# Two attention layers on 32 images: second layer normalised before its product, with a new order of work

## The reference

```
# layer 0, for each image
h    = group_norm(x, 32 groups) * gn_w + gn_b
q,k,v = split(qkv_w @ h + qkv_b)            # 128 x 1024 each
attn = softmax(q.T @ k * C**-0.5)           # 1024 x 1024
x1   = x + proj_w @ (v @ attn.T) + proj_b
# layer 1
q = Wq @ x1 + bq ; k = Wk @ x1 + bk         # 16 x 1024 each
v = Wv @ x1 + bv                            # 128 x 1024
y = gamma * (v @ softmax(q.T @ k).T) + x1
```

## Time and profile before

| | |
|---|---|
| median of three runs | 1635.73 us (1635.26 to 1635.94) |
| profiled execution, own time | 1633.07 us |
| its span, first to last instruction | 1630.8 us |
| granted TensorE clock, mean | 0.988 |
| busy share PE / DVE / ACT / POOL | 93% / 79% / 74% / 76% |
| DMA moved | 305 MB, 187 GB/s over the span |

### The profile page before, as it was taken

How to read it: one execution, slowest core, us unless ns; L and a number is a source line. 1 busy time by engine, 2 the same in 40 slices (tenths; PEclk the granted TensorE clock), 3 DMA queues, 4 the chain that set the end, 5 groups by cost and what they waited for, 6 DMA issues and landing times.

```text
span 1630.8 us, 43555 instructions
## 1 busy us (share of the span) xinstructions
PE 1519.8 (93%) x16777; PEld 1102.4 (68%) x16777; DVE 1289.7 (79%) x2499; ACT 1209.0 (74%) x1697; POOL 1247.4 (76%) x1036
## 2 busy tenths in 40 slices
PE   3789999999999999999999999999999999999975
PEld 1557777767777677776767777677677777767754
DVE  2478888888888888888888888888888888887854
ACT  1467887777777777777777777877777877777753
POOL 3998888887888887787888788788878888877600
PEclk9999999999999999999999999999999999999987
DMA  1689999999999999999999999999999999999974
GB/s 47 117 143 200 196 198 201 209 192 201 195 201 204 198 196 196 197 198 192 203 203 204 203 190 204 198 198 205 190 203 194 195 205 197 203 189 186 195 137 97
DMA packets 1081437, 305.19 MB, mean 187 GB/s; under 512 B 1068273, under 2 KB 1068945, under 8 KB 1081233
## 3 DMA queue, kind: packets, MB, share of 16 engines
q1 hardware_dynamic: 1080080, 302.41, 106.1%
q10 hardware_dynamic: 1152, 0.00, 0.0%
HBM read 17.13 MB, written 16.78 MB: 21 GB/s over the span
## 4 chain that ended last, share of the span: by engine, by line
PE 48%; ACT 22%; DVE 16%; issue 10%; POOL 2%; DMA 1%; SPq 1%; ACTq 0%; POOLq 0%; DVEq 0%
DVE nmax L498 10%; ACT scores L402 9%; ACT prob L397 8%; PE mixed L710 7%; PE mixed L712 7%; PE mixed L711 7%; PE scores L671 6%; PE bank_w L778 4%; PE scores L673 4%; PE scores L672 4%; PE scores L696 3%; PE bank_t L731 2%; ACT v_head L452 2%; PE bank_w L768 2%; DVE qk L563 1%
## 5 line engine op out<-in xcount | busy, mean ns | idle before, releaser
L710 PE MATMUL mixed<-v_head,pt 128*128 128x129 f16 x4096 | 722.6, 223 | 4.5 <-DMA pt<-rows 4.3
L712 PE MATMUL mixed<-v_head,pt 128*128 128x129 f16 x4096 | 722.5, 220 | 0.0
L711 PE MATMUL mixed<-v_tail,pt 128*128 128x128 f16 x4096 | 722.2, 219 | 0.0
L498 DVE TENSOR_REDUCE nmax<-scores 128x1 f32<-128x1024 f32 x512 | 602.4, 1216 | 52.6 <-PE scores L696 32.3
L305 POOL TENSOR_TENSOR rows<-prob,rows 128x1024 f16<-128x1024 f32 x256 | 545.5, 2131 | 21.3
L402 ACT ACTIVATE scores<-scores,nmax 128x1024 f32<-128x1024 f32 x256 | 278.6, 1088 | 279.4 <-DVE nmax L498 279.4
L300 POOL TENSOR_SCALAR rows<-prob 128x1024 f16<-128x1024 f32 x256 | 267.9, 1046 | 227.3 <-ACT prob L397 210.8
L512 DVE SCALAR_TENSOR_TENSOR rows<-scores,rows 128x1024 f16<-128x1024 f32 x256 | 313.6, 1225 | 153.3 <-ACT rows L409 153.2
L711 PEld LDWEIGHTS mixed<-v_tail,pt 128*128 128x128 f16 x4096 | 407.0, 99 | 2.7
L710 PEld LDWEIGHTS mixed<-v_head,pt 128*128 128x128 f16 x4096 | 400.2, 98 | 7.0 <-DMA pt<-rows 6.6
L712 PEld LDWEIGHTS mixed<-v_head,pt 128*128 128x128 f16 x4096 | 398.1, 97 | 0.0
(11 more groups left out here) (90 smaller groups left out, 1847.0 us busy)
## 6 DMA issues: line engine op xcount, KB each, us to landing
x_raw<-in_x_dram SPq DMA_DIRECT2D x32, 512.0 KB, 4.8
out_dram<-y SPq DMA_DIRECT2D x64, 256.0 KB, 3.0
pt<-rows SPq DMA_TRANSPOSE x512, 4.9
w_qkv<-in_L_conv_qkv_w_dram SPq DMA_DIRECT2D x3, 64.0 KB, 3.8
b_qk<-in_L_conv_bk_dram SPq DMA_DIRECT2D x8, 0.1 KB, 1.9
b_qk<-in_L_conv_bq_dram SPq DMA_DIRECT2D x8, 0.1 KB, 1.6
w_proj<-in_L_conv_proj_w_dram SPq DMA_DIRECT2D x1, 64.0 KB, 3.5
w_v<-in_L_conv_Wv_dram SPq DMA_DIRECT2D x1, 64.0 KB, 3.4
```

What stands on the lines that cost most here:

```text
L498: nc.vector.reduce_max(nmax[layer][:, t:t + 1], scores[layer][:, :], AX.X, negate=True).then_inc(maxed[layer], 1)
L710: mm(mixed[l][:, 0:C + 1], head, vh[:, im.p, m, 0:C + 1], start=(m == 0), stop=False)
L711: mm(mixed[l][:, 0:C], head, vt[:, im.p, m, :], start=False, stop=False)
L712: done = mm(mixed[l][:, 0:C + 1], tail, vh[:, im.p, m, 0:C + 1], start=False, stop=(m == TILES - 1))
```

## The change

- **Layer 1 rows are normalised when they are split.** `exponent1` also writes out the row sum; VectorE scales it down by 4096 and takes the reciprocal (`invert1`, two instructions of one column, behind both row maxima); `head_row1` waits for it and uses it as scale, and `tail_row1` does too. Both are issued in two halves of 512 columns, and each half of `score1` waits for its half of the tail before it.
- **Layer 1's product has channels in partitions.** `attend1` has v1 as the stationary side and the rows as the moving side, so `norm` and `back` fall away for layer 1, with the column of ones, and `y_out` adds `x1b` straight to PSUM.
- **Layer 0** keeps both; its turned tile now lands in a free part of `mixed[0]`, and `attend0` of the next tile waits for `x1_done`. `x_bias` and `xb` are gone: `x1_out` adds bias and `x_raw` itself. `x_raw` has five buffers and is loaded earlier.
- **The order** of the list on every engine is new. TensorE: scores 1, scores 0, turn back, attend 1, projections, attend 0, q and k. ScalarE: exponent 1, head 1, the outs of v, qk1 and v1, and only then exponent 0 and norm. VectorE: max 1, max 0, invert 1, exp bias, x1, tail 1, y, the tails, invert 0, group norm. The waits `adds_done` and `evicted_here` on TensorE are gone. In the new list v is in steps 0 and 2, qk1 in 1 and 3, its copies in 3 and 4, v1 in 6 and 7, q and k in 2, 4, 5 and 0, statistics in 4 and 5, group-norm products in 6 and 7, and `h_head` in 7.

The diff, cut; the waits of `qk_project`, `v_project`, `qk1_project` and `gn_product` were fitted to the new order, and `attend0` is `attend` for layer 0.

```diff
+X_BUFS = 5
...
+TURNED = slice(2 * C, 3 * C)
...
+PIECES = 2
...
-SCORE = (-1, 12)
-EXP = (0, 13)
-SWING = (1, 13)
-ATTEND = (3, 16)
-ADD = (4, 17)
-QK_AT = (-5, -4, -3, 0)
-GN_AT = (-10, -9)
-V_AT = (1, 2)
-QK1_AT = (7, 11)
-V1_AT = (12, 14)
-TURNED = (slice(0, C), slice(C, 2 * C))
-FIRST_IT, LAST_IT = -2, IMAGES + 2
+LOAD_X, STATS, GN_AT, ROOT_AT = -22, (-20, -19), (-18, -17), -12
+H_FULL, H_HEAD, H_TAIL = -9, -9, -7
+QK_AT, QK_SPLIT = (-6, -4, -3, 0), (-5, -3, -2, 2)
+V_AT, QK1_AT, QK1_COPY, V1_AT = (0, 2), (9, 11), (11, 12), (14, 15)
+EXP, SWING, ATTEND, BACK = (0, 13), (1, 13), (3, 16), 4
+X1_BIAS, STORE = 12, (20, 24)
+FIRST_IT, LAST_IT = -3, IMAGES + 2
...
             def load_x(im):
-                if im.at_least(2):
-                    sp.wait_ge(x_biased, im.n - 1)
-                    sp.wait_ge(h32_done, im.n - 1)
-                    sp.wait_ge(h_head_done, im.n - 1)
-                sp.dma_start(x_raw[:, im.p, :], x_img[im.n]).then_inc(x_loaded[im.p], 16)
+                if im.at_least(X_BUFS):
+                    sp.wait_ge(x1_done, (im.n - X_BUFS + 1) * TILES)
+                sp.dma_start(x_raw[:, im.n % X_BUFS, :], x_img[im.n]).then_inc(x_loaded[im.n % X_BUFS], 16)
...
-            def x_bias(im):
-                if isinstance(im.n, int) and im.n == 0:
-                    pool.wait_ge(setup_dve, SETUP_DVE_ALL)
-                if im.at_least(2):
-                    pool.wait_ge(x1_done, im.n * TILES - TILES)
-                    stand_apart()
-                nc.gpsimd.tensor_scalar(xb[:, im.p, :], x_raw[:, im.p, :], bias0[:, 0:1], 1.0, ALU.add,
-                                        ALU.mult).then_inc(x_biased, 1)
...
             def exponent1(im, t):
                 act.wait_ge(maxed[1], im.n * TILES + t + 1)
                 nc.scalar.activation(scores[1][:, :], scores[1][:, :], ACT.Exp,
-                                     bias=nmax[1][:, t:t + 1], scale=1.0).then_inc(exped[1], 1)
+                                     bias=nmax[1][:, t:t + 1], scale=1.0,
+                                     accum_out=rsum[:, t:t + 1]).then_inc(exped[1], 1)
 
             def head_row1(im, t):
                 if early := two_before(im, t):
                     act.wait_ge(swung[1][early[1] % RING], swings(*early))
-                act.wait_ge(exped[1], im.n * TILES + t + 1)
-                nc.scalar.activation(rows[1][:, t % 2, 0, :], scores[1][:, :], ACT.Copy,
-                                     scale=P_UP).then_inc(row_headed[1], 1)
-
-            def norm(l, im, t):
-                act.wait_ge(inverted[l], im.n * TILES + t + 1)
-                nc.scalar.activation(normal[l][:, :], mixed[l][:, 0:C], ACT.Copy,
-                                     scale=rinv[l][:, t:t + 1]).then_inc(normed[l], 1)
+                act.wait_ge(inverted[1], im.n * TILES + t + 1)
+                for piece in range(PIECES):
+                    cols = slice(piece * N // PIECES, (piece + 1) * N // PIECES)
+                    nc.scalar.activation(rows[1][:, t % 2, 0, cols], scores[1][:, cols], ACT.Copy,
+                                         scale=rinv[1][:, t:t + 1]).then_inc(row_headed[1], 1)
+
+            def norm(im, t):
+                act.wait_ge(inverted[0], im.n * TILES + t + 1)
+                nc.scalar.activation(normal[:, :], mixed[0][:, 0:C], ACT.Copy,
+                                     scale=rinv[0][:, t:t + 1]).then_inc(normed, 1)
...
-                        if im := at(it, k, QK1_AT[h] + 1):
+                        if im := at(it, k, QK1_COPY[h]):
                             qk1_copy(im, h)
                     if tile := tile_at(it, k, EXP[1]):
                         exponent1(*tile)
                         head_row1(*tile)
-                    if tile := tile_at(it, k, EXP[0]):
-                        exponent0(*tile)
...
+                    if tile := tile_at(it, k, EXP[0]):
+                        exponent0(*tile)
+                    if tile := tile_at(it, k, ATTEND[0]):
+                        norm(*tile)
...
-                    if im := at(it, k, -7):
+                    if im := at(it, k, H_HEAD):
                         h_head_out(im)
-                    for l in range(2):
-                        if tile := tile_at(it, k, ATTEND[l]):
-                            norm(l, *tile)
...
 
-            def invert(l, im, t):
-                dve.wait_ge(attended[l], im.n * TILES + t + 1)
-                nc.vector.reciprocal(rinv[l][:, t:t + 1], mixed[l][:, C:C + 1]).then_inc(inverted[l], 1)
+            def invert0(im, t):
+                dve.wait_ge(attended[0], im.n * TILES + t + 1)
+                nc.vector.reciprocal(rinv[0][:, t:t + 1], mixed[0][:, C:C + 1]).then_inc(inverted[0], 1)
+
+            def invert1(im, t):
+                dve.wait_ge(exped[1], im.n * TILES + t + 1)
...
+                                        ALU.mult).then_inc(lowered, 1)
+                dve.wait_ge(lowered, im.n * TILES + t + 1)
+                nc.vector.reciprocal(rinv[1][:, t:t + 1], rsum_down[:, t:t + 1]).then_inc(inverted[1], 1)
 
...
-                dve.wait_ge(row_headed[1], im.n * TILES + t + 1)
-                nc.vector.scalar_tensor_tensor(out=rows[1][:, t % 2, 1, :], in0=scores[1][:, :], scalar=P_UP,
-                                               in1=rows[1][:, t % 2, 0, :], op0=ALU.mult,
-                                               op1=ALU.subtract).then_inc(row_tailed[1], 1)
+                for piece in range(PIECES):
+                    cols = slice(piece * N // PIECES, (piece + 1) * N // PIECES)
+                    dve.wait_ge(row_headed[1], (im.n * TILES + t) * PIECES + piece + 1)
+                    nc.vector.scalar_tensor_tensor(out=rows[1][:, t % 2, 1, cols], in0=scores[1][:, cols],
+                                                   scalar=rinv[1][:, t:t + 1], in1=rows[1][:, t % 2, 0, cols],
+                                                   op0=ALU.mult, op1=ALU.subtract).then_inc(row_tailed[1], 1)
 
             def x1_out(im, t):
                 cols = slice(t * C, (t + 1) * C)
-                if t == 0:
...
-                nc.vector.tensor_tensor(x1[:, im.p, cols], bank_t[:, TURNED[0]], xb[:, im.p, cols],
-                                        ALU.add).then_inc(x1_done, 1)
+                dve.wait_ge(turned, im.n * TILES + t + 1)
+                if t == 0 and im.at_least(2):
+                    dve.wait_ge(x1_biased, im.n - 1)
+                nc.vector.scalar_tensor_tensor(out=x1[:, im.p, cols], in0=mixed[0][:, TURNED], scalar=bias0[:, 0:1],
+                                               in1=x_raw[:, im.n % X_BUFS, cols], op0=ALU.add,
+                                               op1=ALU.add).then_inc(x1_done, 1)
...
                 h, cols = t // PER_HALF, slice(t * C, (t + 1) * C)
+                dve.wait_ge(attended[1], im.n * TILES + t + 1)
...
-                nc.vector.tensor_tensor(y[:, h, (t % PER_HALF) * C:(t % PER_HALF + 1) * C], bank_t[:, TURNED[1]],
-                                        x1b[:, im.p, cols], ALU.add).then_inc(y_done, 1)
+                nc.vector.scalar_tensor_tensor(out=y[:, h, (t % PER_HALF) * C:(t % PER_HALF + 1) * C],
+                                               in0=mixed[1][:, 0:C], scalar=1.0 / P_UP, in1=x1b[:, im.p, cols],
+                                               op0=ALU.mult, op1=ALU.add).then_inc(y_done, 1)
...
                 for k in range(8):
-                    if tile := tile_at(it, k, EXP[1]):
-                        row_max(1, *tile)
+                    here = tile_at(it, k, EXP[1])
+                    if here:
+                        row_max(1, *here)
                     if tile := tile_at(it, k, EXP[0]):
                         row_max(0, *tile)
+                    if here:
+                        invert1(*here)
+                    if tile := tile_at(it, k, EXP[0]):
                         exp_bias(*tile)
-                    for l in range(2):
-                        if tile := tile_at(it, k, ADD[l]):
-                            dve.wait_ge(turned[l], tile[0].n * TILES + tile[1] + 1)
-                    if tile := tile_at(it, k, ADD[0]):
+                    if tile := tile_at(it, k, BACK):
                         x1_out(*tile)
-                    if tile := tile_at(it, k, ADD[1]):
+                    if here:
+                        tail_row1(*here)
+                    if tile := tile_at(it, k, ATTEND[1]):
                         y_out(*tile)
-                    if tile := tile_at(it, k, EXP[1]):
-                        tail_row1(*tile)
-                    for l in range(2):
-                        if tile := tile_at(it, k, ATTEND[l]):
-                            invert(l, *tile)
                     for h in range(2):
                         if im := at(it, k, V_AT[h]):
...
-                        if im := at(it, k, -12 + h):
+                    if tile := tile_at(it, k, ATTEND[0]):
+                        invert0(*tile)
...
```

(51 more changed lines are left out.)

143 lines of the change are left out of this document (66 added, 77 removed).

## The result

The changed kernel takes 1672.6 us (1671.95 to 1673.29, four runs) beside 1635.49 us for the one before: a ratio of 1.0227, with a 95% interval of 1.021 to 1.0245. It is slower by 37.1 us. The forecast was slower, 1654 us, by 18.5; direction and range hold, the size is half of what came.

What follows compares the result with a forecast made beforehand. Light steps were bound by a ring of maxima, exponentials and head, projection steps by TensorE. The new ring adds 0.64 us an image, + 19 over some 30 images, + 1 for the ends: 1654 us, range 1606 to 1678.

Steps and rivals of the forecast that it cites:

- The ring: Chain from maxima through `invert1`, `head_row1` and `exponent0` back: 5.33 us; through layer 1's tail and `exponent1`: 5.43 plus read-out.
- T: The moment at which VectorE starts `invert1`, behind both maxima, 1.13 us after the start of max 0.
- the outs ahead of `exponent0`: ScalarE's copies of v, qk1 and v1: no waiting, but 0.49 us added for v and v1, 0.66 for qk1.
- the three copies of step 2: On ScalarE, `norm`, the copy of q and k and `qk1_copy` delay the next step's `exponent1`; step forecast at 6.11 us.
- the ends: Layer 1 alone at the end: 0.1 to 0.2 us more in each of 16 steps, last tile saves about 1; together + 1.
- The pointer: On ScalarE's head, taking the scale from a column costs up to 0.09 us; 0.08 was taken.
- The read-out a: Writing out the row sum after `exponent1` on ScalarE: estimated 0.16 us, bounds nothing to 0.36.
- a = 0: Rival: reading out the row sum costs nothing; 47.68 us an image, 1629 us; chance 0.13.
- A full instruction (0.36): Rival: reading out the row sum costs a full instruction with its wait; 50.01 us an image, 1699 us; chance 0.06.
- Late turned tiles: Rival: GpSimd's waits for the DMA move to ScalarE's head, 0.70 us an image; 1675 us; chance 0.11.
- TensorE gives back its turns: Rival: TensorE is the bound and 28 us of turns back are won; 1608 us; chance 0.19.
- The limit: With SyncE's queue waiting 22.8 of 800 us and transfers unchanged, time can't fall by more than 2.9%, to 1589.

Runs made afterwards that it cites:

- the short copy: Changed kernel with the first of two copies of layer 1 queries (L422) cut to 64 of 512 columns, save for the first two images: 1662.27 us.
- the half swings: Layer 1's transpose cut to the head rows: in the changed kernel without normalising, 1584.74 us; in the kernel before, 1635.32 us.
- the never normalised kernel: Changed kernel with constant 4096 as scale of head and tail, no wait for `invert1`, which is left out: 1612.96 us.

## Why the direction was right and the size half

**The ring, right.** The structure stood as forecast: `head_row1` waits for `invert1` in all steps, TensorE is busy for 45.99 of 49.09 us (94%, forecast under 95%), steps are 5.87 to 6.37 us. `exponent0` to max 0 was 1.56 and is 1.56; max 0 to T 1.13 and is 1.15. Five of the eight steps agree within 0.07: 7, 0, 4, 5 and 6 with 6.11, 5.91, 5.87, 6.14 and 6.28 against 6.14, 5.87, 5.92, 6.21 and 6.30; step 1 is 0.09 over, 6.08 against 5.99.

**The term that failed: the outs ahead of `exponent0` in step 3.** The prediction took all of them as unable to wait ("TensorE has made them about 1.1 us after T"). For the second `qk1_project` this is wrong: its product ends 1.84 us after T. It needs the last `x1_out`, which the same change put behind `invert1`, and TensorE's new list has it ahead of `attend0`, where both `attend`s stood before it in the old one. Of the 0.88 us of wait some 0.6 come of standing behind `invert1`, an estimate: VectorE waits 0.35 us for `exponent1` before it, and `x1_out` starts 0.32 after T. The step was 5.99 in the list and is 6.37, + 0.38. Shown by taking the wait away: - 0.28 in that step, 9.7 us in all.

**The second: the three copies of step 2.** The list had 6.11 with `norm`, the copy of q and k and `qk1_copy` making `exponent1` late; it is 6.33. `norm` waits 0.28 us for `invert0` there and starts at T + 3.47. Elsewhere an instruction on ScalarE starts some 0.1 us before the end of the one ahead of it (820.68 and 0.60, then 821.16), and so I had them; neither the copy of the queries (L422) nor the exponential behind it does (822.83 and 0.68, then 823.53; and 0.63, then 824.18). Why not wasn't settled. VectorE waits 0.35 for `exponent1` there, 16 times in 800 us, 5.7 us. Shown by the short copy: - 0.38 in that step, 10.3 us in all.

Steps 3 and 2 are 0.38 and 0.22 over, all others together 0.04 under: 0.56 for a regular image.

**Luck in the count of images.** The prediction multiplied by 30 and added 1 for the ends, and 30 times 1.20 plus 1 is the 37.1 us measured. The traces show another sum. Only 27 images take the regular 49.1 us, so the two steps explain 27 times 0.56 = 15 of the 18.6 us missed. The second image of the ramp, in which layer 1 begins, takes 4.7 us more than before, and the prediction gave it no term of its own. The changed kernel and the one before, from `exponent0` of that image's first tile to that of the next image's:

```profile
75.11:122.01 46.90, 36.15 (x363) 25.05 (x364) 30.32 (x66) 29.58 (x46) 39.82 (x33) 1.00 0.78 143
75.20:117.38 42.18, 35.99 (x346) 23.34 (x344) 27.87 (x53) 27.61 (x37) 40.66 (x34) 1.00 0.90 152
```

The first image of the ramp is 0.5 us shorter, the last two that are followed by another are 1.4 us longer together, and what comes behind them 1.1. Which part of the change makes the ramp longer wasn't settled.

**Smaller terms.** `invert1` with its handoffs is 0.44 to 0.45 to the head instead of 0.39. Halves take 1.16 instead of 1.14. TensorE's busy time fell by 0.6 us an image, where eight turns of 0.11 are 0.9; why wasn't settled. That "no engine waits for GpSimd" overlooks, where SyncE waits 16.7 us for its rows; the half swings show that this wait held nothing before. The pointer costs 0.09 on a whole head (1.11 against 1.02), with 0.08 forecast. The read-out a was 0.16 and is 0.12: `exponent1` ends at 825.27, its read-out at 825.39.

**The rivals.** a = 0 is refuted by a row, an instruction of 0.19 us, whose whole cost in the kernel is 14.3 us. The Trainium skill (VectorE: DVE Perf Modes, "Two Vector instructions with no wait between them") states of VectorE that an operation which also writes out its accumulator is two instructions. The trace shows the same on ScalarE, and no run here shows it for VectorE. The list gave 0.85 us an image for a = 0.16, or 25 us. Less came because a is 0.12 and counts in four steps only; in the other four the kernel without the read-out is no faster. A full instruction (0.36) is refuted by the same row. Late turned tiles did not come: no wait for the DMA is in the view. That TensorE gives back its turns is refuted for this kernel: it idles more. The limit that the prediction put on this rival, 1589 us with all of the queue's 22.8 us of waits given back, wasn't reached: with no wait left, the never normalised kernel stands at 1613. Single images of it come to the 46.5 us that 2.9% less would be (46.40 is the shortest), others take 48.5. A transpose stays on the queue hardly longer than before, by the median 2.45 us against 2.41 (400 to 1200 us). What makes the long images long wasn't settled; that the queue holds the kernel there is shown by the half swing.

**Where the expected gain went.** With the rows left unnormalised the new list takes 1613 us; whether the turns' TensorE time, ScalarE's second `norm`, GpSimd's `x_bias` or the order gives it wasn't tried apart. It is lost to a wait of 0.53 us in each step, two one-column instructions and a read-out in the only chain that had no slack.

## What to carry to other kernels

Work moved from behind a product to ahead of it goes from an engine's free time onto the ring that sets its steps: find that ring first, and add up the new links with their handoffs. When an order is rewritten, check each job on the ring for inputs that the same change has made later; one such wait, in one of eight steps, was 0.38 us an image of this error, and a run of copies ahead of a critical exponential 0.22. Look at the ramp too, and not only at the regular images: one image of it was 4.7 us of the loss. A large instruction between two engines of a ring can be cut in two even where each pair of halves takes its engine longer (1.27 us against 1.11 on ScalarE, 1.41 against 1.28 on VectorE): here it was worth 60 us.

## What the hardware showed that was not expected

An exponential on ScalarE with a row sum is followed by an instruction of its own, 0.19 to 0.20 us, which ends 0.12 us after the exponential. A copy of 64x512 float16 on ScalarE (L422) started 0.02 us after the end of the instruction ahead of it, and the exponential behind it 0.02 us after the copy's, where other neighbours overlap by 0.1. A queue that issues nothing but transposes of 512 KB and an image's load and stores had no wait in the never normalised kernel, and yet images with the same 16 transposes took it between 46.4 and 48.5 us; before, at an even 47.9 us, it had 1.4 us of waits an image (22.8 of 800 us). And work taken from that queue is worth 28 us or nothing, by what else holds the kernel: 1613 to 1585 us in one, 1634.7 to 1635.3 in the other.
